# Three routing steps behind the gatings of blocks 11 to 13, in a fused attention and expert kernel

## The reference: linear attention, then routed experts

```
q, k = exp(x Wq + bq), exp(x Wk + bk)          # 16 heads of 8 channels
out  = (q . cumsum(k v)) / (q . cumsum(k))      # causal, per head
x1   = layernorm(x + out Wo + bo)
scores = sigmoid(x1 gate_w)                     # 32 experts in 4 groups of 8
choice = scores + gate_bias
keep the 2 groups whose two best choices sum highest, in them the 8 best experts
weight = scores of those 8 / their sum * 2.5
y  = sum_e weight_e * down_e(silu(gate_e x1) * up_e x1) + shared expert
out = layernorm(x1 + y)
```

## Time and profile before

| | us |
|---|---|
| three runs | 454.15, 813.19, 451.9 |
| median of the three | 454.15 |
| profiled execution, its own time | 450.73 |
| its span | 448.9 |
| TensorE busy in the span | 425.8 (95%) |
| VectorE busy | 340.7 (76%) |
| GpSimd busy | 302.6 (67%) |
| ScalarE busy | 275.6 (61%) |

### The profile page before, as it was taken

One profiled execution on the slowest core, in us unless ns is written; L12 is line 12 of the kernel. 1 busy time (PEld: TensorE's weight loads), 2 busy tenths in 40 slices (PEclk: granted clock), 3 DMA queues, 4 the chain that ended last, 5 costly groups with the idle time before them and its releaser, 6 DMA issues.

```text
span 448.9 us, 10927 instructions
## 1 busy us (share of the span) xinstructions
PE 425.8 (95%) x4000; PEld 327.6 (73%) x4000; DVE 340.7 (76%) x905; ACT 275.6 (61%) x536; POOL 302.6 (67%) x225
## 2 busy tenths in 40 slices
PE   7888999999999999999999999999999999989992
PEld 5766877778777887778776887778777786666771
DVE  3767896896778697796878777886967968768644
ACT  4755558744887359754696358863697447554642
POOL 3554668836967578855878369664878467777791
PEclk9999999999999999999999999999999999999997
DMA  8400845255234545045354544245461542237400
GB/s 284 171 1 21 195 100 119 61 116 129 75 77 101 118 96 140 26 107 131 75 117 101 115 100 96 54 95 118 95 142 50 120 104 70 66 98 177 112 20 23
DMA packets 28885, 45.10 MB, mean 100 GB/s; under 512 B 2080, under 2 KB 10656, under 8 KB 28448
## 3 DMA queue, kind: packets, MB, share of 16 engines
q1 hardware_dynamic: 28544, 44.14, 41.1%
q10 hardware_dynamic: 288, 0.26, 0.2%
HBM read 41.77 MB, written 2.62 MB: 99 GB/s over the span
## 4 chain that ended last, share of the span: by engine, by line
DVE 34%; PE 31%; POOL 14%; issue 11%; ACT 3%; DVEq 1%; ACTq 0%; POOLq 0%
PE bank L379 29%; POOL units L1136 9%; DVE units L979 8%; POOL hidden_lo L1176 3%; DVE hidden_lo L846 3%; DVE stats L866 3%; DVE top_of_group L907 2%; DVE bank L900 2%; DVE x L878 2%; DVE probs L856 2%; ACT hidden_hi L697 2%; DVE replaced L939 1%; DVE out_sb L1043 1%; DVE bank L1061 1%; DVE mean_var L871 1%
## 5 line engine op out<-in xcount | busy, mean ns | idle before, releaser
L1136 POOL TENSOR_TENSOR units<-units,weight_wide 128x512 f32<-128x512 f32 x127 | 175.7, 1389 | 101.6 <-DVE units L979 92.3
L697 ACT ACTIVATE hidden_hi<-units 128x512 fp32r<-128x512 f32 x136 | 85.8, 632 | 65.5 <-POOL units L1136 62.2
L979 DVE TENSOR_TENSOR units<-bank,units 128x512 f32<-128x512 f32 x136 | 92.3, 683 | 32.3 <-PE bank L379 21.2
L716 ACT ACTIVATE units<-bank 128x512 f32<-128x512 f32 x136 | 80.1, 590 | 57.8 <-PE bank L379 57.2
L846 DVE TENSOR_TENSOR hidden_lo<-units,hidden_hi 128x512 fp32r<-128x512 f32 x103 | 90.8, 883 | 23.6 <-ACT hidden_hi L697 23.5
L379 PE MATMUL bank<-x_hi,gate_hi 128*128 128x512 f32 x136 | 61.1, 450 | 1.2 <-ACT units L716 0.5
L379 PE MATMUL bank<-x_hi,up_hi 128*128 128x512 f32 x136 | 56.1, 412 | 2.6 <-ACT units L716 2.6
L379 PE MATMUL bank<-hidden_hi,down_hi 128*128 128x512 f32 x136 | 54.5, 400 | 2.3 <-POOL hidden_lo L1176 1.9
L379 PE MATMUL bank<-x_lo,gate_hi 128*128 128x512 f32 x136 | 53.9, 397 | 0.0
L379 PE MATMUL bank<-x_hi,gate_lo 128*128 128x512 f32 x136 | 53.9, 396 | 0.0
L379 PE MATMUL bank<-x_hi,up_lo 128*128 128x512 f32 x136 | 53.8, 396 | 0.0
(11 more groups left out here) (129 smaller groups left out, 694.5 us busy)
## 6 DMA issues: line engine op xcount, KB each, us to landing
weight_wide<-weight_d SPq DMA_DIRECT2D x60, 512.0 KB, 6.7
x_tok<-x_in SPq DMA_DIRECT2D x8, 256.0 KB, 6.8
xT<-xT_in SPq DMA_DIRECT2D x7, 256.0 KB, 6.7
out_dram<-out_sb SPq DMA_DIRECT2D x7, 256.0 KB, 2.3
weight_wide<-up_in SPq DMA_DIRECT2D x1, 1088.0 KB, 6.8
up_raw<-up_in SPq DMA_DIRECT2D x1, 1088.0 KB, 8.9
down_raw<-down_in SPq DMA_DIRECT2D x1, 1088.0 KB, 7.8
weight_wide<-weight_d SPq DMA_DIRECT2D x8, 128.0 KB, 3.1
```

Of the source, the lines that this page charges most:

```text
L697: nc.scalar.activation(hidden_hi[place(n, g)][:, :], units[place(n, g)][:, :], ACT.Copy).then_inc(hidden_hi_done, 1)
L716: nc.scalar.activation(units[place(n, g)][:, :], banks[up_bank(2 * n, g)][:, :], ACT.Silu).then_inc(silu_done, 1)
L979: V.tensor_tensor(units[place(n, g)][:, :], banks[up_bank(2 * n + 1, g)][:, :], units[place(n, g)][:, :], ALU.mult).then_inc(gated_done, 1)
L1136: G.tensor_tensor(units[place(n, g)][:, :], units[place(n, g)][:, :], weight_wide[:, w % (2 * PIECE), :], ALU.mult).then_inc(hidden_done, 1)
```

## The change

It has three parts. For the routing of groups m = 1 to 6, each of the three VectorE steps is issued one slot later: the first behind the gating of block 11, the second behind that of block 12, the third behind that of block 13. For the same groups, TensorE turns the weights in slot 15, between up(15) and down(11), where it did so in slot 14 ahead of gate(15); ScalarE's copy to `weightT` moves to slot 15 as well. For group m = 7 TensorE and ScalarE already did so, and its VectorE steps stay. In the last group (g = 7) ScalarE copies y of group 6 ahead of the high part of block 2, where it did so behind it.

```diff
@@ TensorE, slot
                 if ffn:
                     up(n, g, u)
-                if m == GROUPS - 1 and n == 15:
+                if mid and m > 0 and n == 15:
                     turn_weights(m)
...
-                if mid and n == 14 and m < GROUPS - 1:
+                if m == 0 and mid and n == 14:
                     turn_weights(m)
@@ ScalarE, slot
+            def copy_y(t):
+
+                act.wait_ge(down_done, reached(BLOCKS * (t + 1)))
+                act.wait_ge(y_turned, reached(t))
+                for c in (HALVES if t == GROUPS - 1 else (slice(0, GROUP),)):
+                    nc.scalar.activation(yT[:, c], y_bank[:, c], ACT.Copy).then_inc(y_copied, 1)
...
-                if tail and n == 4:
-                    t = g - 1
...
+                if tail and n == 4 and g != GROUPS - 1:
+                    copy_y(g - 1)
...
-                if mid and n == (14 if m < GROUPS - 1 else 15):
+                if mid and n == (14 if m == 0 else 15):
                     act.wait_ge(weight_turned, reached(m + 1))
...
+                if g == GROUPS - 1 and n == 3:
+                    copy_y(g - 1)
                 if ffn:
                     for b in ready_blocks(n, g):
                         high_part(b, g)
@@ VectorE, slot
-                if mid and n == 10:
+                later = 1 if 0 < m < GROUPS - 1 else 0
+                if mid and n == 10 + later:
                     expert_scores(m)
                     group_tops(m)
-                if mid and n == 11:
+                if mid and n == 11 + later:
                     masked_experts(m)
-                if mid and n == 12:
+                if mid and n == 12 + later:
                     expert_weights(m)
```

## The result

The changed kernel is slower, as forecast: a median of 462.38 us (462.29 to 462.54, 4 runs) against 451.9 us for the kernel before beside it (451.17, 451.9 and 454.15). The ratio is 1.023, with a 95% interval of 1.0188 to 1.0273. The profiled execution took 462.54 us, its span is 460.8 us against 448.9. A fourth run of the kernel before, 813.19 us, lies far from the others and is not compared.

A forecast was written before the change was run, and what follows sets the result against it. TensorE was taken as the bound, busy 51.42 of 51.83 us a group. Six groups' later denominators added 13.4 us and the copy of y zero to 450.73, giving 464.1 us; forecast's own range 461 to 467.5, overall range 453 to 468.

The forecast's parts named there:

- Part 1: VectorE's routing steps: gating 11 waits for the silu of block 11, so the weights are done 3.55 us later.
- Part 2: TensorE's list: gate(14) 0.7 us later, 1.2 us wait for the turned weights, down(11) 1.5 us later.
- TensorE's own sum: TensorE's delay in group 3 from its own waits, after 0.2 us comes back at the denominators: 1.4 us.
- Part 3: GpSimd's product with q, behind the product of block 15, ends last and puts group 3's denominators 2.05 us later.
- The rival in which only TensorE's own waits count: GpSimd's product with q is in time at the denominators: 9.6 us more, 460.3 us; chance 0.17.
- Part 4: Earlier copy of y in the last group: between 0.5 us gained and 0.5 lost, taken as zero.
- The signs: New profile's expected marks: VectorE idle some 3 us before gating 11, TensorE about 1.2 before the weights, groups about 54.
- fourth rival: Weight loads also land late, delaying GpSimd's first routed product: another 1.35 us a group, 472 us; chance 0.08.
- second rival: Most of the delay is absorbed by TensorE's hidden waits, leaving 0.6 us a group: 454.5 us; chance 0.20.

The follow-up runs named there:

- steps alone: Kernel before with only the three VectorE steps one slot later in groups 1 to 6, weights still turned in slot 14: 471.32 us, ratio 1.0466.
- third alone: Kernel before with only the third VectorE step one slot later and the weights turned in slot 15: 448.53 us, ratio 0.9939.
- two late: Kernel before with the second and third VectorE steps one slot later and the weights turned in slot 15: 447.9 us, ratio 0.9929.
- q first: Changed kernel with GpSimd's product with q ahead of its product of block 15: 461.37 us, ratio 1.0209 to the kernel before.
- two late with the turning in slot 14: Kernel before with the second and third VectorE steps one slot later, weights still turned in slot 14: 452.56 us, ratio 1.0025.

## Why the prediction was right, and where it was off

- **Part 1 held.** From the start of gating 11 to the weights 10.8 us were forecast and 10.95 measured; gatings 12 and 13 came 4.0 and 2.87 us behind one another as replayed. The experiments without exponentials and with the first step early show that the silu is the cause.
- **Part 2 held.** Forecast 1.2 us of waiting for the weights in group 3, measured 1.22; and 0.7 later at gate(14), where the trace has 0.59 idle. TensorE's own sum was 1.4 for that group, the measured growth 1.64. Of the 0.2 us that should have come back at the denominators, less did: from down(11) to there it takes 6.54 us (246.91 to 253.45), before 6.60 (239.38 to 245.98), and 0.1 of that is the first wide matmul behind the turning, which advances by 0.32 in place of 0.22.
- **Part 3 was mis-sized, and this is the step that failed.** The product with q was taken at its 1.75 us of before, and it was to set the denominators, for 2.05 us in group 3. It took 1.31. It still ended last, but only by 0.05 us; without it TensorE's own list would have come to nearly the same place. From silu to denominators 18.45 us were forecast and 18.0 measured (235.44 to 253.45). The error lies in a reading of the rows. The prediction took the long one of the two products before as that of block 15, beside the low part of block 14; it was that of block 14, beside the low part of block 13, and the low part of block 14 had lengthened the product with q. So when this low part came to stand beside the product of block 15, that one became long and the product with q short, and the sum counted it in both. With 1.31 in place of 1.75 the sum is 10.8 us for six groups; 10.7 were measured and 13.4 forecast. The rival in which only TensorE's own waits count had 9.6, which is nearer than the forecast. The rule that the prediction takes from the Trainium skill, "SBUF — State Buffer", section "SBUF: two separate sides", also bears on the product with q: that one now has no VectorE instruction with two inputs in SBUF beside it, only the masked scores, which read PSUM. The trace agrees at both places, 1.31 for that product, and 1.68 for the product of block 15, beside which the low part of block 14 had started 0.17 us sooner and kept its 0.68.
- **Part 4 held.** The copy of y was taken at zero, and measured 0.9995.
- **The total** of 464 us against 462.38 is nearer than part 3 deserves, by luck. The sum went from one profiled execution, 450.73, to 464.1, and the changed kernel's took 462.54. Part 3 was 2.7 us too high, and 1.1 us came that no part had: 0.3 ahead of the first changed slot and 0.8 behind the last gate. The mean in the sum, too, is 2.23 and not 2.25; the 13.4 are right for it. In ratios, 1.0296 was forecast and 1.023 measured; the interval reaches down to 1.0188, just below 2%. Beside 23 runs of the kernel before, the change without the copy has 1.0241, with a lower end of 1.0206.
- **The signs** were met but for two sizes. VectorE idles 4.04 us before gating 11 and not some 3: the sum's 2.95 come on top of the 1.09 that it idled already. The wait for the product with q at the denominators is 0.05 us. A middle group takes 53.47 us, where about 54 was written.
- **The loads** (fourth rival) did come late enough to release GpSimd's first product: after the denominators at 253.45 it starts 3.75 us later, before 3.60 (249.58 - 245.98), and in the six groups 3.7 to 4.2 later. The rival's sign was there and its cost was not: the stretch from 199.98 to 253.45 holds the latest of these starts (204.16), TensorE is idle in it for 1.98 us, and 1.86 of them are the waits at gate(14), at the weights and at the denominators.
- **The absorption** (second rival) is excluded: the groups take 53.3 to 53.7 us, above the 52.5 of its sign.

## What to carry to other kernels

A step that moves behind another is not the same work in another order when the one ahead of it waits for somebody: ask what the engine does in the wait that it uncovers. Here the first of three steps stood in a gap that closed with it, so its place was free, while the second and third stood in nobody's gap and belonged behind the gatings; the best version takes two of the three, and needs the consumer's place in the list moved with them. When durations are taken over into a replay, look at what ran beside them: a row may be long because of its neighbour, and the length does not move with the row.

## What the runs showed of the hardware

The same GpSimd product of 128x512 values (`k_sum` with `qT`) took 1.75 us in the kernel before and 1.31 us in the changed one; the product of block 15 took 1.28 and 1.68, the other way round. The traces of seven kernels of this study (before, changed, steps alone, third alone, two late, q first, two late with the turning in slot 14) have 1176 GpSimd instructions of this shape and kind. With no VectorE instruction with two inputs in SBUF beside them, 700 took 1.26 to 1.32 us, also where a gating or masked scores ran beside them. Where such a VectorE instruction came second, 228 took the same, and VectorE's up to 2.37 in place of 0.68. Where it had started first, 248 took 1.28 to 1.82, with a median of 1.66.

A turning of four small matmuls between wide ones, found ready, advances TensorE by 0.35 us, and the first wide matmul behind it by 0.32 in place of 0.23 us.
